# Attention of layer 0: exponentials first in ScalarE's round, conversions of the outputs last, projections in the rounds without a query

## The chip, the cores and the metric

The kernel runs on one core of one Trainium2 chip. A core has TensorE (PE, matrix multiplication), VectorE (DVE), ScalarE (ACT), GpSimd (POOL) and SyncE (SP, which issues transfers). The metric is the device time of one execution in microseconds (us). Each engine works through its own list of instructions in the order in which they were written, and waits at semaphores for the others.

## The reference

Two transformer layers over 4 sequences of 256 tokens with 512 features. The change touches the attention of layer 0 alone:

```
q_c = x @ Wq_c.T + bq_c;          q = q_c @ Wq_up.T + bq_up            # 32 heads
kv_nope, kv_rope = split(x @ Wkv_c.T + bkv_c)
k_nope, v = split(kv_nope @ Wkv_up.T + bkv_up);  k = [k_nope, kv_rope]
attn = softmax(q @ k.T / sqrt(192))                                    # 256 x 256 per sequence and head
out  = sum over heads of (attn @ v) @ Wo.T + bo
```

After it come a layernorm, a gated feed-forward, a second attention and a second feed-forward, which stay as they are.

## The kernel before

`attention0_heads` computes the 32 heads (h), each for 4 sequences (b = 0 to 3). One pair of h and b is a step s = 4h + b, and one round handles one step, as a software pipeline: in round s every engine does work that belongs to steps s + 1, s, s - 1, s - 2 and s - 3. Each engine has its own `round_(h, b)`, and the order of the calls in it is the order of its instructions. There is no scheduler. A hardware loop repeats heads 2 to 30; heads 0, 1, 31 and the rounds behind the last head stand outside it.

What one step goes through:

- TensorE `scores(s)` writes the bank `bs` (two of them). VectorE `maxes` (L548) takes the negative row maxima, ScalarE `exps` (L492) two exponentials with their row sums.
- VectorE `inverse` (L553) takes the reciprocals, GpSimd `norm` (L462) multiplies, TensorE `turn` (L635) transposes into `bt` (two banks).
- ScalarE `probs` (L498) copies the high part out of `bt`, VectorE `probs` (L557) computes the low part `pt_lo`.
- TensorE `values` (L646) multiplies with the latent values into `bo`, of which there is one bank. Steps 0 and 1 of a head make one pair, steps 2 and 3 the next.
- ScalarE `outs` (L503) copies the high part of a finished pair, VectorE `outs` (L562) makes the low part. Only after that may `values` of the next pair overwrite `bo`: it waits for `s_olo`.
- TensorE `project` (L655, L657) adds the pair to the accumulator; SyncE duplicates a part of `o_hi` for it by DMA.

Two queries per head are made for two sequences each: `merge` (L601, L603) and its conversions (L529, L532, L483, L537) prepare one matrix for a head; TensorE `query` makes `bq`, ScalarE `query` (L487) the high part, VectorE `query` (L542) the low part, which `scores` waits for.

In every round VectorE begins with the reciprocals of step s - 1 and the maxima of step s. ScalarE ends its round with the exponentials of step s. In rounds 1 and 3 of a head both have the outputs of a finished pair ahead of `probs`; in round 3 VectorE also does one reduction for a later layer (L585, "part"). TensorE has `project` in rounds 1 and 3, and a `query` in the same rounds.

Of the kernel before, what the change touches and what calls it, by code (L numbers as in the profile page):

```python
# [46 lines left out]
NH = 32  # L47
# [17 lines left out]
def f32(ap):  # L65

    return ap.bitcast(F32)
# [17 lines left out]
def plain(eng, sem):  # L85


    eng.sem_inc(sem, 1)


def has(x, n):

    return not isinstance(x, int) or 0 <= x < n
# [236 lines left out]
def attention0_heads(nc, k, io, g, lat, acc, first):  # L330
# [10 lines left out]
    NS, NPAIR = NB * NH, 2 * NH  # L341
    with ExitStack() as ctx:
# [35 lines left out]
        def run(eng, round_):  # L378

            def head(h):  # L380
                for b in range(NB):
                    round_(h, b)

            head(0)
            head(1)
            with eng.Fori(2, NH - 1) as h:
                head(h)
            head(NH - 1)
            head(NH)
            round_(NH + 1, 0)  # L390
            round_(NH + 1, 1)

        with nc.Block() as block:
            @block.sync
# [40 lines left out]
            @block.gpsimd  # L435
            def _(pool):
                def rope_part(h):


                    pool.wait_ge(s_w, 16 * h + 16)  # L440
                    need(pool, s_glo, h)
                    need(pool, s_qlo, 2 * h)
                    plain(pool, s_tick)
                    pool.tensor_scalar(gm[:, :, KVL:P], rope, SCALE0, None, ALU.mult)
                    pool.tensor_scalar(gb[:, :], bcols[:, 1:2], SCALE0, None, ALU.mult).then_inc(s_gpool, 1)

                def split_wv(h):
                    pool.wait_ge(s_wv, 16 * h + 16)
                    need(pool, s_om, 2 * h)
                    plain(pool, s_tick)  # L450
                    pool.tensor_copy(wvs[0][:, :], wv[:, :]).then_inc(s_wvh, 1)
                    pool.wait_ge(s_wvh, h + 1)
                    plain(pool, s_tick)
                    pool.tensor_copy(wvs[1][0:KVL, :], wv[0:KVL, :]).then_inc(s_wvl, 1)
                    pool.wait_ge(s_wvl, 2 * h + 1)
                    pool.tensor_tensor(wvs[1][KVL:P, :], wv[KVL:P, :], f32(wvs[0][KVL:P, :]), ALU.subtract)\
                        .then_inc(s_wvl, 1)
                    pool.wait_ge(s_wvl, 2 * h + 2)

                def norm(s, b):  # L460
                    pool.wait_ge(s_inv, s + 1)
                    pool.tensor_tensor(pr[b][:, :, :], pr[b][:, :, :],  # L462
                                       rinv[b][:, :][:, :, None].to_broadcast([P, 2, S]), ALU.mult)\
                        .then_inc(s_norm, 1)

                def round_(h, b):
                    s = 4 * h + b
                    if has(s - 1, NS):
                        norm(s - 1, (b - 1) % 4)
                    if b == 0 and has(h + 1, NH):  # L470
                        rope_part(h + 1)
                    if b == 2 and has(h - 1, NH):
                        split_wv(h - 1)

                rope_part(0)
                run(pool, round_)

            @block.scalar
            def _(act):
                def merged(h):  # L480
                    act.wait_ge(s_graw, h + 1)
                    act.wait_ge(s_gpool, h + 1)
                    act.activation(gms[0][:, :, :], gm[:, :, :], ACT.Identity).then_inc(s_ghi, 1)  # L483

                def query(p, par):
                    act.wait_ge(s_qmm, p + 1)
                    act.activation(q[par][0][:, :], bq[:, :], ACT.Identity, bias=gb[:, :]).then_inc(s_qhi, 1)  # L487

                def exps(s, b):
                    act.wait_ge(s_max, s + 1)  # L490
                    for i in range(2):
                        m = act.activation(pr[b][:, i, :], bs[b % 2][:, i * S:(i + 1) * S], ACT.Exp,  # L492
                                           bias=nmax[b][:, i:i + 1], accum_out=rsum[b][:, i:i + 1])
                    m.then_inc(s_exp, 1)

                def probs(s, b):
                    act.wait_ge(s_tmm, s + 1)
                    act.activation(pt[b][0][:, :, :], bt[b % 2][:, :].rearrange("p (a n) -> p a n", a=2),  # L498
                                   ACT.Identity).then_inc(s_thi, 1)

                def outs(p, par):
                    act.wait_ge(s_pv, 2 * p + 2)
                    act.activation(o[par][0][:, :], bo[:, :], ACT.Identity).then_inc(s_ohi, 1)  # L503

                def round_(h, b):
                    s = 4 * h + b
                    if b == 0 and has(2 * h + 1, NPAIR) and not (isinstance(h, int) and h == 0):
                        query(2 * h + 1, 1)
                    if b == 2 and has(2 * h + 2, NPAIR):
                        query(2 * h + 2, 0)  # L510
                    if b % 2 and has(2 * h - 2 + b // 2, NPAIR):
                        outs(2 * h - 2 + b // 2, b // 2)
                    if b == 1 and has(h + 1, NH):
                        merged(h + 1)
                    if has(s - 2, NS):
                        probs(s - 2, (b - 2) % 4)
                    if has(s, NS):
                        exps(s, b)

                merged(0)  # L520
                query(0, 0)
                query(1, 1)
                run(act, round_)

            @block.vector
            def _(dve):
# [28 lines left out]
                def probs(s, b):  # L555
                    dve.wait_ge(s_thi, s + 1)
                    dve.tensor_tensor(pt[b][1][:, :, :], bt[b % 2][:, :].rearrange("p (a n) -> p a n", a=2),  # L557
                                      f32(pt[b][0][:, :, :]), ALU.subtract).then_inc(s_tlo, 1)

                def outs(p, par):  # L560
                    dve.wait_ge(s_ohi, p + 1)
                    dve.tensor_tensor(o[par][1][0:KVL, :], bo[0:KVL, :], f32(o[par][0][0:KVL, :]), ALU.subtract)\  # L562
                       .then_inc(s_olo, 1)

                def round_(h, b):
                    s = 4 * h + b
                    if has(s - 1, NS):
                        inverse(s - 1, (b - 1) % 4)
                    if has(s, NS):
                        maxes(s, b)  # L570
                    if b == 1 and has(h + 1, NH):
                        merged_raw(h + 1)
                    if b == 0 and has(2 * h + 1, NPAIR) and not (isinstance(h, int) and h == 0):
                        query(2 * h + 1, 1)
                    if b == 2 and has(2 * h + 2, NPAIR):
                        query(2 * h + 2, 0)
                    if b % 2 and has(2 * h - 2 + b // 2, NPAIR):
                        outs(2 * h - 2 + b // 2, b // 2)
                    if b == 1 and has(h + 1, NH):
                        merged_lo(h + 1)  # L580
                    if has(s - 2, NS):
                        probs(s - 2, (b - 2) % 4)
                    if b == 3 and has(h, NH):
                        dve.wait_ge(s_part, 16 * h + 16)
                        dve.tensor_reduce(g["mag"][:, bass.ds(h, 1)], part[:, :], AX, ALU.max,  # L585
                                          apply_absolute_value=True).then_inc(s_mag, 1)
# [8 lines left out]
            def _(pe):  # L595
# [64 lines left out]
                def round_(h, b):  # L660
                    s = 4 * h + b
                    if has(s + 1, NS):
                        scores(s + 1, 2 * h + (b + 1) // 2, (b + 1) % 4)
                    if b == 3 and has(h + 1, NH):
                        query(h + 1, 2 * h + 3, 1)
                    if b == 1 and has(h - 2, NH):
                        project(h - 2, 2 * h - 3, 1)
                    if b == 3 and has(h - 1, NH):
                        project(h - 1, 2 * h - 2, 0)
                    if has(s - 1, NS):  # L670
                        turn(s - 1, (b - 1) % 4)
                    if has(s - 3, NS):
                        values(s - 3, 2 * h + (b - 3) // 2, (b - 3) % 4)
                    if b == 0 and has(h + 1, NH):
                        merge(h + 1)
                    if b == 1 and has(h + 1, NH):
                        query(h + 1, 2 * h + 2, 0)
# [1198 lines left out]
```

## Time and profile before

| | |
|---|---|
| median of 3 runs | 1572.85 us (1572.0 to 1576.03) |
| the profiled execution | 1576.75 us |
| its span, first to last instruction | 1575.0 us |
| busy over the span | PE 95%, PEld 83%, DVE 70%, ACT 49%, POOL 31% |
| granted TensorE clock, mean | 0.982 of full speed |

The stage of the 32 heads lies between 41.6 us (its first exponential) and about 409 us. In the slices of the page, where each digit is the busy share of a fortieth of the span in tenths, it covers slices 2 to 10. TensorE is busy in nine tenths or more there, ScalarE and VectorE in seven to eight tenths. Rows of a timeline have the start, the duration, the engine, the line and the operation, and in brackets the idle time of the engine just before it and who ended it. The start of one instruction and that of the next on the same engine can lie closer together than the duration says, since they overlap; a chain is followed by starts.

### The profile page before, as it was taken

Reading aid. Unit: us, or ns where it says so; the run is one execution under the profiler, and the core shown is the slowest. Engines: PE = TensorE matmul, PEld = TensorE weight load, DVE = VectorE, ACT = ScalarE, POOL = GpSimd, SP = SyncE. Lnnn points to the kernel's source line nnn. Section 1 sums busy time; section 2 is a strip of 40 time slices with the busy share of each in tenths; the row PEclk is TensorE's granted clock in tenths of the full one; section 3 lists DMA queues with packets and bytes.
Section 4 is the critical chain, followed back from the end, with each engine's and each line's share of the span. In section 5 each row is a group of like instructions: output and inputs, shape, how many; then the busy total and the mean of one; then the engine's idle time right before and its main releaser. Section 6 shows DMA issues by size and latency. Waiting matters only on the chain. (4 is left out here: it accounts for less than half of the span.)

```text
span 1575.0 us, 29365 instructions
## 1 busy us (share of the span) xinstructions
PE 1496.1 (95%) x8993; PEld 1312.2 (83%) x8993; DVE 1099.8 (70%) x2790; ACT 767.7 (49%) x2153; POOL 484.6 (31%) x537
## 2 busy tenths in 40 slices
PE   6999999999689989999999999999999999999898
PEld 5888888888368777988888888888888888988776
DVE  3788888888576756676676666666666666666666
ACT  3777777777345534444434444344443444434421
POOL 3455555555230113123213213312311321320321
PEclk9999999999889999999999999999999999999999
DMA  4222222222245440110011011011011101100001
GB/s 159 66 69 74 71 73 73 73 73 69 69 121 154 127 160 1 54 55 24 29 53 53 0 53 53 0 53 53 11 42 53 46 7 53 53 0 14 1 14 41
DMA packets 47954, 88.60 MB, mean 56 GB/s; under 512 B 6064, under 2 KB 14768, under 8 KB 47920
## 3 DMA queue, kind: packets, MB, share of 16 engines
q1 hardware_dynamic: 47920, 88.16, 19.1%
q8 instruction: 19, 0.31, 0.1%
q14 instruction: 15, 0.12, 0.0%
HBM read 77.66 MB, written 2.10 MB: 51 GB/s over the span
## 5 line engine op out<-in xcount | busy, mean ns | idle before, releaser
L98 PE MATMUL c_bj<-g_xT_hi,b_w 128*128 128x512 f32 x512 | 214.7, 419 | 2.8 <-PEq L928 2.8
L99 PE MATMUL c_bj<-g_xT_lo,b_w 128*128 128x512 f32 x512 | 203.5, 397 | 0.0
L100 PE MATMUL c_bj<-g_xT_hi,b_w 128*128 128x512 f32 x512 | 203.1, 397 | 0.0
L462 POOL TENSOR_TENSOR h_pr<-h_pr,h_rinv 128x512 f32<-128x512 f32 x128 | 133.2, 1041 | 152.9 <-DVE h_rinv L553 150.4
L1146 POOL CAST b_w<-b_raw_q 128x512 fp32r<-128x512 f32 x32 | 20.5, 640 | 435.8 <-PE c_bj L100 435.8
L98 PE MATMUL c_bj<-b_w,g_xT_hi 128*128 128x256 f32 x512 | 143.4, 280 | 0.0
L99 PE MATMUL c_bj<-b_w,g_xT_hi 128*128 128x256 f32 x512 | 143.2, 280 | 0.0
L100 PE MATMUL c_bj<-b_w,g_xT_lo 128*128 128x256 f32 x512 | 142.7, 279 | 0.0
L1378 DVE TENSOR_TENSOR c_v_lo<-c_bj,c_v_hi 128x256 fp32r<-128x256 f32 x128 | 54.3, 424 | 94.0 <-ACT c_v_hi L1290 94.0
L1382 DVE TENSOR_TENSOR g_res<-c_bj,g_res 128x512 f32<-128x512 f32 x128 | 88.3, 691 | 45.4 <-PE c_bj L100 42.8
L492 ACT ACTIVATE h_pr<-h_bs,h_nmax 128x256 f32<-128x256 f32 x256 | 118.8, 475 | 2.1 <-DVE h_nmax L548 2.1
L1274 ACT ACTIVATE c_o<-c_bo 128x128 f32<-128x128 f32 x128 | 35.5, 278 | 171.7 <-PE c_bo L1492 171.7
L100 PEld LDWEIGHTS c_bj<-g_xT_hi,b_w 128*128 128x128 f32 x512 | 97.1, 190 | 23.3
L98 PEld LDWEIGHTS c_bj<-g_xT_hi,b_w 128*128 128x128 f32 x512 | 97.1, 190 | 20.6 <-issue 3.3
L99 PEld LDWEIGHTS c_bj<-g_xT_lo,b_w 128*128 128x128 f32 x512 | 97.6, 191 | 17.2
L1269 ACT ACTIVATE c_pt<-c_bt 128x384 fp32r<-128x384 f32 x128 | 62.9, 491 | 90.0 <-PE c_bt L1479 90.0
L1290 ACT ACTIVATE c_v_hi<-c_bj 128x256 fp32r<-128x256 f32 x128 | 49.2, 384 | 116.6 <-PE c_bj L100 116.6
L98 PE MATMUL c_bj<-b_w,c_oT_hi 128*128 128x512 f32 x256 | 100.9, 394 | 2.1 <-DVEq L1386 2.1
L100 PE MATMUL c_bj<-b_w,c_oT_lo 128*128 128x512 f32 x256 | 100.3, 392 | 0.0
L99 PE MATMUL c_bj<-b_w,c_oT_hi 128*128 128x512 f32 x256 | 100.2, 391 | 0.0
L98 PEld LDWEIGHTS c_bj<-b_w,g_xT_hi 128*128 128x128 f32 x512 | 96.3, 188 | 3.0
L99 PEld LDWEIGHTS c_bj<-b_w,g_xT_hi 128*128 128x128 f32 x512 | 96.4, 188 | 2.9
(265 smaller groups left out, 4639.4 us busy)
## 6 DMA issues: line engine op xcount, KB each, us to landing
f_wi<-in_w_ffn SPq DMA_DIRECT2D x66, 256.0 KB, 2.6
h_part<-in_w_ffn SPq DMA_DIRECT2D x32, 264.0 KB, 2.6
h_o_mix<-h_o_hi SPq DMA_DIRECT2D x64, 128.0 KB, 2.2
b_raw_q<-in_w_attn SPq DMA_DIRECT2D x32, 256.0 KB, 6.4
b_raw_k<-in_w_attn SPq DMA_DIRECT2D x32, 256.0 KB, 7.0
b_raw_v<-in_w_attn SPq DMA_DIRECT2D x16, 512.0 KB, 7.4
b_raw_o<-in_w_attn SPq DMA_DIRECT2D x16, 512.0 KB, 3.9
a_w<-in_w_head SPq DMA_DIRECT2D x32, 225.0 KB, 2.6
```

The lines of the kernel that those rows point to most:

```text
L98: pe.matmul(out, w[0], x[0], start=start, stop=False, skip_group_check=True)
L99: pe.matmul(out, w[0], x[1], start=False, stop=False, skip_group_check=True)
L100: return pe.matmul(out, w[1], x[0], start=False, stop=stop, skip_group_check=True)
L462: pool.tensor_tensor(pr[b][:, :, :], pr[b][:, :, :], rinv[b][:, :][:, :, None].to_broadcast([P, 2, S]), ALU.mult)\
L492: m = act.activation(pr[b][:, i, :], bs[b % 2][:, i * S:(i + 1) * S], ACT.Exp, bias=nmax[b][:, i:i + 1], accum_out=rsum[b][:, i:i + 1])
L1146: pool.tensor_copy(hi[:, :], self.raw[n][:, :]).then_inc(self.s_whi[n], 1)
L1269: act.activation(pt[0], bt[:, 0:3 * P], ACT.Identity).then_inc(s_thi, 1)
L1274: act.activation(o1[:, :], bo[t % 2][:, 2 * P:3 * P], ACT.Identity).then_inc(s_orest, 1)
L1290: act.activation(v[c][0][:, 2 * t + bank - 1, :], bj[bank][:, 0:2 * DV], ACT.Identity)\
L1378: dve.tensor_tensor(lo, bj[bank][:, 0:2 * DV], f32(hi), ALU.subtract).then_inc(s_jlo[bank], 1)
L1382: dve.tensor_tensor(res[:, j, :], bj[bank][:, :], res[:, j, :], ALU.add)\
```

## The change

ScalarE's round begins with the exponentials of its step and no longer ends with them. On ScalarE and VectorE the outputs of a pair come after `probs`. The projections of a head move one round later each: from round 3 and the next head's round 1 to rounds 0 and 2 (those without a `query`). GpSimd's `split_wv` moves from round 2 to round 3, and a third round is added behind the last head. No arithmetic is added or taken away.

```
@@ (the rounds behind the last head)
-            round_(NH + 1, 0)
-            round_(NH + 1, 1)
+            for b in range(3):
+                round_(NH + 1, b)
@@ GpSimd
-                    if b == 2 and has(h - 1, NH):
+                    if b == 3 and has(h - 1, NH):
                         split_wv(h - 1)
@@ ScalarE, round_(h, b)
+                    if has(s, NS):
+                        exps(s, b)
                     (query)
-                    if b % 2 and has(2 * h - 2 + b // 2, NPAIR):
-                        outs(2 * h - 2 + b // 2, b // 2)
                     (merged)
                     if has(s - 2, NS):
                         probs(s - 2, (b - 2) % 4)
-                    if has(s, NS):
-                        exps(s, b)
+                    if b % 2 and has(2 * h - 2 + b // 2, NPAIR):
+                        outs(2 * h - 2 + b // 2, b // 2)
@@ VectorE, round_(h, b)
-                    if b % 2 and has(2 * h - 2 + b // 2, NPAIR):
-                        outs(2 * h - 2 + b // 2, b // 2)
                     (merged_lo)
                     if has(s - 2, NS):
                         probs(s - 2, (b - 2) % 4)
+                    if b % 2 and has(2 * h - 2 + b // 2, NPAIR):
+                        outs(2 * h - 2 + b // 2, b // 2)
@@ TensorE, round_(h, b)
-                    if b == 1 and has(h - 2, NH):
-                        project(h - 2, 2 * h - 3, 1)
-                    if b == 3 and has(h - 1, NH):
-                        project(h - 1, 2 * h - 2, 0)
+                    if b % 2 == 0 and has(h - 2, NH):
+                        project(h - 2, 2 * h - 4 + b // 2, b // 2)
```

ScalarE inside the loop, rounds 2 and 3 of a head, before. L487 is a query, L492 the exponentials, L503 the outputs of a pair, L498 `probs`; the digit in a name is the buffer.

```order
L487 ACTIVATE h_q0_hi<-h_bq,h_gb 128x512 [waits a_q_mm]
L498 ACTIVATE h_pt0_hi<-h_bt0 128x512 [waits a_t_mm]
L490 REGISTER_ALU
L492 ACTIVATE h_pr2,h_rsum2<-h_bs0,h_nmax2 128x256 [waits a_s_max]
L492 ACTIVATE h_pr2,h_rsum2<-h_bs0,h_nmax2 128x256
L502 ISA
L503 ACTIVATE h_o1_hi<-h_bo 128x512 [waits a_pv]
L498 ACTIVATE h_pt1_hi<-h_bt1 128x512 [waits a_t_mm]
L490 REGISTER_ALU
L492 ACTIVATE h_pr3,h_rsum3<-h_bs1,h_nmax3 128x256 [waits a_s_max]
L492 ACTIVATE h_pr3,h_rsum3<-h_bs1,h_nmax3 128x256
```

The same two rounds now:

```order
L492 ACTIVATE h_pr2,h_rsum2<-h_bs0,h_nmax2 128x256 [waits a_s_max]
L492 ACTIVATE h_pr2,h_rsum2<-h_bs0,h_nmax2 128x256
L486 REGISTER_ALU
L487 ACTIVATE h_q0_hi<-h_bq,h_gb 128x512 [waits a_q_mm]
L498 ACTIVATE h_pt0_hi<-h_bt0 128x512 [waits a_t_mm]
L490 REGISTER_ALU
L492 ACTIVATE h_pr3,h_rsum3<-h_bs1,h_nmax3 128x256 [waits a_s_max]
L492 ACTIVATE h_pr3,h_rsum3<-h_bs1,h_nmax3 128x256
L498 ACTIVATE h_pt1_hi<-h_bt1 128x512 [waits a_t_mm]
L502 ISA
L503 ACTIVATE h_o1_hi<-h_bo 128x512 [waits a_pv]
```

The wait for the maxima (`a_s_max`) now stands ahead of `probs`, and the outputs stand behind it.

VectorE in the loop, rounds 2 and 3 of a head, before. L553 are the reciprocals, L548 the maxima, L562 the outputs, L557 `pt_lo`.

```order
L553 RECIPROCAL h_rinv1<-h_rsum1 128x2 [waits a_s_exp]
L547 REGISTER_ALU
L548 TENSOR_REDUCE h_nmax2<-h_bs0 128x2 [waits a_s_mm]
L541 REGISTER_ALU
L542 SCALAR_TENSOR_TENSOR h_q0_lo<-h_bq,h_gb,h_q0_hi 128x512 [waits a_q_hi]
L557 TENSOR_TENSOR h_pt0_lo<-h_bt0,h_pt0_hi 128x512 [waits a_t_hi]
L553 RECIPROCAL h_rinv2<-h_rsum2 128x2 [waits a_s_exp]
L547 REGISTER_ALU
L548 TENSOR_REDUCE h_nmax3<-h_bs1 128x2 [waits a_s_mm]
L562 TENSOR_TENSOR h_o1_mix<-h_bo,h_o1_hi 64x512 [waits a_o_hi]
L557 TENSOR_TENSOR h_pt1_lo<-h_bt1,h_pt1_hi 128x512 [waits a_t_hi]
```

Round 3 there now, from its reciprocals:

```order
L553 RECIPROCAL h_rinv2<-h_rsum2 128x2 [waits a_s_exp]
L547 REGISTER_ALU
L548 TENSOR_REDUCE h_nmax3<-h_bs1 128x2 [waits a_s_mm]
L557 TENSOR_TENSOR h_pt1_lo<-h_bt1,h_pt1_hi 128x512 [waits a_t_hi]
L562 TENSOR_TENSOR h_o1_mix<-h_bo,h_o1_hi 64x512 [waits a_o_hi]
```

On VectorE the exchange of L562 and L557 is all; reciprocals and maxima still open the round.

## Rows read from the trace of the kernel before

**Rows 1.** Busy time of each engine from the first exponential to the stage's end.
```profile
41.60:409.30 367.70, 342.99 (x2402) 309.05 (x2401) 297.95 (x634) 272.89 (x797) 188.27 (x286) 1.00 0.27 70
```
**Rows 2.** Instructions that touch h_pr: the exponentials, first and last start.
```profile
L492 ACT ACTIVATE h_pr<-h_bs,h_nmax x256: 457/474/508, 41.6 to 399.1; 128x256 f32<-128x256 f32 x128
```
**Rows 3.** Waits between 60 and 380 us: total, times, longest.
```profile
PEld h_bs L98 <- ACT h_pr L492: 21.3, 28, 0.8
```
**Rows 4.** Timeline of one head, round 3: ScalarE, VectorE and TensorE's first product.
```profile
308.28 0.22 ACT L492 ACTIVATION_READ_ACCUMULATOR h_pr<-h_bs,h_nmax 128x1 f32 x1
308.37 0.61 ACT L503 ACTIVATE h_o_hi<-h_bo 128x512 fp32r<-128x512 f32 x1
308.53 0.17 DVE L553 RECIPROCAL h_rinv<-h_rsum 128x2 f32<-128x2 f32 x1
308.55 0.39 PE L98 MATMUL h_bs<-a_kv_hi,h_q_hi 128*128 128x256 f32 x1 [0.56 <-ACT h_pr L492]
...
309.23 0.67 DVE L562 TENSOR_TENSOR h_o_mix<-h_bo,h_o_hi 64x512 fp32r<-64x512 f32 x1
...
309.83 0.67 DVE L557 TENSOR_TENSOR h_pt_lo<-h_bt,h_pt_hi 128x512 fp32r<-128x512 f32 x1
...
310.17 0.21 ACT L492 ACTIVATION_READ_ACCUMULATOR h_pr<-h_bs,h_nmax 128x1 f32 x1
...
310.43 0.68 DVE L585 TENSOR_REDUCE g_mag<-h_part 128x528 int32 x1
...
311.04 0.15 DVE L553 RECIPROCAL h_rinv<-h_rsum 128x2 f32<-128x2 f32 x1
```
**Rows 5.** The same timeline, a query on TensorE and round 2.
```profile
305.06 0.39 PE L98 MATMUL h_bq<-a_qa_hi,h_gm_hi 128*128 128x512 f32 x1
...
306.21 0.28 PE L98 MATMUL h_bs<-a_kv_hi,h_q_hi 128*128 128x256 f32 x1
...
306.41 0.69 ACT L487 ACTIVATE h_q_hi<-h_bq,h_gb 128x512 fp32r<-128x512 f32 x1 [1.24 <-PE h_bq L615]
...
307.00 0.59 ACT L498 ACTIVATE h_pt_hi<-h_bt 128x512 fp32r<-128x512 f32 x1
307.13 0.75 DVE L542 SCALAR_TENSOR_TENSOR h_q_lo<-h_bq,h_gb,h_q_hi 128x512 fp32r<-128x512 f32 x1 [1.14 <-ACT h_q_hi L487]
...
307.47 0.48 ACT L492 ACTIVATE h_pr<-h_bs,h_nmax 128x256 f32<-128x256 f32 x1
...
307.80 0.68 DVE L557 TENSOR_TENSOR h_pt_lo<-h_bt,h_pt_hi 128x512 fp32r<-128x512 f32 x1
```
**Rows 6.** The same timeline, round 1: the conversion of the merged matrix.
```profile
303.36 0.42 ACT L483 ACTIVATE h_gm_hi<-h_gm 128x256 fp32r<-128x256 f32 x1 [0.38 <-DVE h_gb L532]
...
303.69 0.58 ACT L498 ACTIVATE h_pt_hi<-h_bt 128x512 fp32r<-128x512 f32 x1
```
**Rows 7.** Timeline of head 0, where exponentials wait for the maxima.
```profile
48.23 0.17 DVE L553 RECIPROCAL h_rinv<-h_rsum 128x2 f32<-128x2 f32 x1
48.31 0.67 DVE L548 TENSOR_REDUCE h_nmax<-h_bs 128x2 f32<-128x512 f32 x1
...
49.01 0.47 ACT L492 ACTIVATE h_pr<-h_bs,h_nmax 128x256 f32<-128x256 f32 x1 [0.33 <-DVE h_nmax L548]
```
**Rows 8.** Timeline behind the last head: values that wait for the outputs.
```profile
403.29 0.68 DVE L562 TENSOR_TENSOR h_o_mix<-h_bo,h_o_hi 64x512 fp32r<-64x512 f32 x1 [2.36 <-ACT h_o_hi L503]
...
404.12 0.36 PE L646 MATMUL h_bo<-h_pt_hi,a_cs 128*128 128x256 f32 x1 [1.03 <-DVE h_o_mix L562]
...
404.66 0.35 PE L646 MATMUL h_bo<-h_pt_hi,a_cs 128*128 128x256 f32 x1
```
**Rows 9.** Stretches where TensorE was less busy, columns as in rows 1; clock last but two.
```profile
398.66:402.07 3.41, 1.71 (x13) 1.51 (x14) 2.26 (x5) 1.54 (x6) 1.22 (x2) 1.00 0.23 58
...
405.49:408.90 3.41, 1.30 (x4) 0.60 (x4) 0.68 (x1) 0.50 (x1) 0.00 (x0) 1.00 0.17 38
408.90:412.31 3.41, 2.74 (x5) 1.25 (x5) 0.33 (x2) 2.83 (x4) 0.00 (x0) 0.50 0.55 167
```

## The prediction

> **What bounds the kernel now.** I read the busy time of the stage first, then the waits in it, then the timeline of one head. Between 41.60 and 409.30 us TensorE is busy for 342.99 of 367.70 us at the full clock, VectorE for 297.95 and ScalarE for 272.89 [rows 1]. The first exponential of the stage starts at 41.6 us and the last step's at 399.1 [rows 2]: 357.5 us for 127 rounds, 2.815 us a round, 11.26 us a head. So TensorE carries the stage, and what it waits for is what a better order could give back. In the waits there is one such line: the weight load of `scores` waits for the exponentials once per head, 21.3 us over 28 heads, 0.76 us each [rows 3]. In the timeline it is round 3: the exponentials of round 2 end at 308.28 + 0.22 = 308.50, and the product starts at 308.55 [rows 4]. The exponentials are that late because they stand behind the query, which starts at 306.41, and `probs`, at 307.00 [rows 5]. This is the wait that exponentials in front take away. TensorE's own work is then 11.26 - 0.76 = 10.5 us a head.
>
> **The stall that goes.** With the exponentials in front and 0.45 us of projection moved into round 2, nothing of the 0.76 us need be left: at most 0.76 x 31.75 heads (127 rounds) = 24 us. This is the upper bound of the gain, and it is only had if the other engines keep up.
>
> **What the new order adds.** Look at what stands between two maxima on VectorE. Its round is reciprocals, maxima of step s, (query or merged matrix), `pt_lo`, (outputs, part). `pt_lo` waits for ScalarE's `probs`. Before, ScalarE did `probs` ahead of the exponentials, so VectorE could do the maxima and go on to `pt_lo` while ScalarE was at its exponentials. Now `probs` stands behind the exponentials, and these wait for the maxima of the same round. So within each round the work is serial: maxima, exponentials, `probs`, `pt_lo`, and only then the next round's reciprocals and maxima. That the exponentials of the next step could start earlier does not help, for their maxima are queued on VectorE behind `pt_lo`.
>
> That a queue is held like this is in the trace: the exponentials of round 3 end at 310.17 + 0.21 = 310.38, and their reciprocals start at 311.04, behind the reduction of "part" that started at 310.43 [rows 4]. The Trainium skill (TensorE: Matmul & The Clock Gate, section on the array's architectural detail) says that ScalarE and VectorE are strict first-in, first-out and TensorE alone reorders, and then only weight loads. By that rule this row is general, and no instruction passes the waiting one; by the opposite the sum would be the gain above. The row agrees with the rule.
>
> **The links**, each from one start to the next:
> - reciprocals to exponentials through the maxima: 49.01 - 48.23 = 0.78 [rows 7]
> - exponentials to the next operation on ScalarE: 308.37 - 307.47 = 0.90 [rows 4, 5]
> - `probs` to `pt_lo`: 0.60 and 0.03 for the semaphore, as from the query's end (306.41 + 0.69 = 307.10) to its low part at 307.13 [rows 5]: 0.63
> - query to its low part: 307.13 - 306.41 = 0.72; low part to `pt_lo`: 307.80 - 307.13 = 0.67 [rows 5]
> - merged matrix to `probs`: 303.69 - 303.36 = 0.33 [rows 6]
> - `pt_lo`, outputs and "part" to the next on VectorE: 0.60, 0.60 and 0.61 [rows 4]
>
> Round 3: 0.78 + 0.90 + 0.63 + 0.60 + 0.60 + 0.61 = 4.12 us. The outputs on ScalarE run beside `pt_lo` and add nothing.
> Round 0: 0.78 + 0.90 + 0.72 + 0.67 + 0.60 = 3.67. `probs` runs beside the query's low part.
> Round 1: 0.78 + 0.90 + 0.33 + 0.63 + 0.60 + 0.60 = 3.84.
> Round 2: as round 0, 3.67, and what the query on TensorE is late.
>
> **TensorE in the new order.** Here the outputs behind `probs` count. `values` of a new pair may start only when the low part of the finished pair is out, which is now the last thing in the same round. In round 1 this low part starts at 0.78 + 0.90 + 0.33 + 0.63 + 0.60 = 3.24 and `values` follow 404.12 - 403.29 = 0.83 later [rows 8], at 4.07; the query behind them 404.66 - 404.12 = 0.54 later, at 4.61; its result reaches ScalarE 306.41 - 305.06 = 1.35 later [rows 5], at 5.96, which is 5.96 - 3.84 = 2.12 in round 2. ScalarE is free at 0.78 + 0.90 = 1.68 there. So round 2 is 3.67 + 0.44 = 4.11.
> In round 3 `values` start at 2.91 + 0.83 = 3.74, while TensorE has been through scores, query and turn by about 2.3; it idles some 1.4 us there and about 2 us ahead of the `values` of round 1. All other waits of TensorE fall inside the 15.7 - 10.5 = 5 us a head in which it has nothing to do, the projections too, which are hidden in any round.
>
> **Sum.** 4.12 + 3.67 + 3.84 + 4.11 = 15.74 us a head instead of 11.26: +4.48 a head, x 31.75 = +142. Head 0 has no outputs and hardly any query to wait for: its four rounds are some 4 us shorter than this, and the last head, without merged matrix and queries, some 2 (0.33, and in round 2 about 1.1, in round 0 nothing): +136. The tail gains the outputs behind one `probs` (0.5). The extra round has only one projection in it, which existed before. SyncE's duplicates start later with the outputs, but their projections come a round later too, and `split_wv` has 5 us of slack a head: nothing for both. Sum so far +137.
>
> **The clock.** In the stage it was 1.00, 2.4 GHz [rows 1]. At the stage's end, where TensorE worked 1.71 of 3.41 us it stayed so; it worked 1.30 of 3.41 us and the next stretch ran at 0.50, which is 1.2 GHz [rows 9]. With 2 us of idleness ahead of the `values` of round 1 the new order is near this. What it costs on the path is the query behind them: 306.21 - 305.06 = 1.15 us [rows 5], becomes 2.3. The bounds are nothing and 1.15 x 31.75 = 37 us. The stretches with 1.7 stand nearer to the new order (10.5 of 15.7 us busy on average), so I take a sixth of the upper end, +6. The Trainium skill (TensorE: Matmul & The Clock Gate, Part 1) has the throttled state as the default that activity releases; by it alone I could not say which of the two holds here, and rows decide.
>
> 1576.75 + 137 + 6 = 1719.75 us for the profiled execution; the median of the runs shown lies 3.9 us below it, so I forecast 1716 us.
>
> **Rivals.**
> 1. *Faster*: VectorE and ScalarE keep ahead of TensorE, the stall of 0.76 goes and nothing takes its place: 1572.85 - 24 = 1549. For it: both are busy for a quarter less than the stage lasts [rows 1], and the exponentials could start before the query. It decides from the point where a round's serial chain is under 2.8 us; the shortest has 3.67. Against: the chain has only links that the trace shows.
> 2. *Only the outputs' wait bites*: VectorE somehow runs ahead, and TensorE loses the 1.4 and 2 us ahead of `values`, less the 0.76: 2.65 x 31.75 = +84, 1657. For it: the place of L503 and L562 is wrong for TensorE whatever the exponentials do. Against: the queue of rows 4.
> 3. *The clock falls in most heads*: the upper end of the term above, and a little more where turns and scores at 1.2 GHz become late: +137 + 37 to 60, 1746 to 1770. If TensorE stayed at 1.2 GHz throughout, its 10.5 us would be 21 a head, over the chain: (21 - 11.26) x 31.75 = +309, 1882. For it: idle stretches of 2 us. Against: busy phases of 3 us and more lie between them.
> 4. *The change doesn't do what it says*: the exponentials stand first but wait there, so nothing starts earlier; with the outputs unhurt the time would stay at 1573. It is true in its first half, and the outputs make the second half unlikely.
>
> **How the numbers follow.** Forecast 0.62 (own range 1695 to 1740: 0.2 us a round are 25 us). Clock in most heads 0.20, at 1.2 GHz throughout 0.03; outputs alone 0.08; faster 0.05; unchanged 0.02. What a measurement can tell is about 0.3%, 5 us. Faster 0.05, same 0.02, slower 0.93. The range 1680 to 1770 leaves out the end of the clock case, the outputs alone and the faster side.
>
> **What would show it.** The starts of L492 should lie 15 to 16.5 us apart per head. ScalarE should be idle ahead of L492 in every round, released by `h_nmax` L548 as in [rows 7], some 1 to 2 us a round, VectorE idle ahead of L557 or L542, released by ScalarE, and TensorE ahead of L646, released by `h_o_mix` L562, twice a head. The wait of L98 for L492 should be gone. I am wrong if L492 still waits for nothing and TensorE stays over 90% busy in the stage, or if the granted clock there is far below 1.

## The result, and the profile after

The changed kernel takes 1748.82 us (median of 4 runs, 1740.43 to 1756.14) against 1573.3: 11.1% more, ratio 1.1111 with a 95% interval of 1.1044 to 1.1179. The forecast was 1716 in a range of 1680 to 1770. The profiled execution took 1742.03 us, 165.3 more than that of before. The four runs lie in two pairs, 1740.43 and 1742.03, and 1755.61 and 1756.14, at mean granted clocks of 0.950, 0.949, 0.952 and 0.953; the trace is of the first pair, and what the other pair's 14 us are is open. All of the 165.3 us has been lost by the time the feed-forward begins: its first product starts at 431.54 us before and at 596.84 after, 165.3 later, and from there to the end both profiles go alike.

One row shows the stage of the heads, from its first exponential to its last. The columns are the length, the busy time of TensorE, its weight loads, VectorE, ScalarE and GpSimd with their counts, the granted clock, the busy share of the DMA engines and GB/s.

```profile
41.60:560.30 518.70, 409.17 (x2372) 344.75 (x2372) 286.81 (x626) 269.48 (x789) 185.07 (x278) 0.89 0.19 49
```

VectorE and ScalarE are busy for about as long as in [rows 1], whose row goes on for 10 us behind the last exponential, but the stage from the first exponential to the last is 161 us longer. Nobody is near its limit: TensorE is busy for 409 of 519 us. The exponentials, against [rows 2]:

```profile
L492 ACT ACTIVATE h_pr<-h_bs,h_nmax x256: 463/473/478, 41.4 to 560.3; 128x256 f32<-128x256 f32 x128
```

From the first to the last it is 518.9 us where it was 357.5: 16.34 us a head instead of 11.26. One exponential lasts as long as before. The waits between 60 and 500 us, with total, times and longest, in place of [rows 3]:

```profile
ACT h_pr L492 <- DVE h_nmax L548: 180.5, 106, 2.1
DVE h_q_lo L542 <- ACT h_q_hi L487: 122.7, 53, 3.6
PE h_bo L646 <- DVE h_o_mix L562: 62.2, 53, 1.5
...
DVE h_pt_lo L557 <- ACT h_pt_hi L498: 42.6, 27, 1.6
...
ACT h_q_hi L487 <- PE h_bq L615: 31.3, 27, 1.8
```

These are the links of the forecast: ScalarE waits for the maxima in every round, VectorE for ScalarE behind them, TensorE for the outputs twice a head. The wait of [rows 3] is not in this list any more. The timeline shows how one round 3 goes, in place of [rows 4]: from the second exponential of round 3 to the first one of the next head's round 0.

```profile
299.65 0.46 ACT L492 ACTIVATE h_pr<-h_bs,h_nmax 128x256 f32<-128x256 f32 x1
...
300.10 0.59 ACT L498 ACTIVATE h_pt_hi<-h_bt 128x512 fp32r<-128x512 f32 x1
...
300.57 0.60 ACT L503 ACTIVATE h_o_hi<-h_bo 128x512 fp32r<-128x512 f32 x1
...
300.72 0.69 DVE L557 TENSOR_TENSOR h_pt_lo<-h_bt,h_pt_hi 128x512 fp32r<-128x512 f32 x1 [1.57 <-ACT h_pt_hi L498]
...
301.33 0.67 DVE L562 TENSOR_TENSOR h_o_mix<-h_bo,h_o_hi 64x512 fp32r<-64x512 f32 x1
...
301.93 0.68 DVE L585 TENSOR_REDUCE g_mag<-h_part 128x528 int32 x1
302.15 0.36 PE L646 MATMUL h_bo<-h_pt_hi,a_cs 128*128 128x256 f32 x1 [0.72 <-DVE h_o_mix L562]
...
302.54 0.15 DVE L553 RECIPROCAL h_rinv<-h_rsum 128x2 f32<-128x2 f32 x1
...
302.61 0.66 DVE L548 TENSOR_REDUCE h_nmax<-h_bs 128x2 f32<-128x512 f32 x1
...
303.31 0.48 ACT L492 ACTIVATE h_pr<-h_bs,h_nmax 128x256 f32<-128x256 f32 x1 [2.13 <-DVE h_nmax L548]
```

VectorE stands idle for 1.57 us until ScalarE, which did its exponentials first, has done `probs`. Then it has `pt_lo`, outputs and "part" ahead of it, and only at 302.54 come reciprocals and maxima. ScalarE in turn has been idle for 2.13 us when it gets the maxima. ScalarE waits for VectorE in every round (106 times in the 27 heads of the list), and VectorE once a round for ScalarE, at L542, L557 or L537, before it gets on to the next maxima.

What the forecast sized wrongly stands in a stretch a little later. First two stretches with their granted clocks, then TensorE in the first of them:

```profile
307.90:314.72 6.82, 5.67 (x20) 4.79 (x21) 2.81 (x6) 3.56 (x11) 1.04 (x1) 0.50 0.22 53
320.00:344.00 24.00, 17.32 (x115) 14.54 (x115) 14.22 (x32) 13.33 (x39) 9.58 (x14) 1.00 0.21 55
```
```profile
307.97 1.11 PE L635 MATMUL h_bt<-g_ident,h_pr 128*128 128x128 f32 x4 [0.45 <-POOL h_pr L462]
...
310.16 0.58 PE L646 MATMUL h_bo<-h_pt_hi,a_cs 128*128 128x256 f32 x1 [1.08 <-DVE h_o_mix L562]
...
311.19 0.63 PE L98 MATMUL h_bq<-a_qa_hi,h_gm_hi 128*128 128x512 f32 x1
...
313.32 0.41 PE L98 MATMUL h_bs<-a_kv_hi,h_q_hi 128*128 128x256 f32 x1
```

At a granted clock of 0.50, 1.2 GHz, the values of round 1 take 1.03 us to the query (0.54 in [rows 8]) and the query 2.13 (1.15 in [rows 5]): 0.49 + 0.98 = 1.47 us more. The `turn` ahead of them (L635) is slow too. In the next head but one, at the full clock, the same two instructions are:

```profile
340.81 0.65 PE L635 MATMUL h_bt<-g_ident,h_pr 128*128 128x128 f32 x4 [0.45 <-POOL h_pr L462]
...
343.00 0.39 PE L646 MATMUL h_bo<-h_pt_hi,a_cs 128*128 128x256 f32 x1 [1.54 <-DVE h_o_mix L562]
```

So the wait ahead of `values` in round 1 is 1.54 us, not 2, and in the slow head the clock fell before it, when TensorE had waited 0.68 us ahead of `merge` (at 305.75) and 0.45 us ahead of `turn`. Of the 20 falls that made a head longer, the clock record of the trace has 12 at this place and 8 behind the wait, in the last of the values or in the query.

The rounds on ScalarE agree. These are the exponentials of rounds 2 and 3, first in this head, then in the next but one, at the full clock:

```profile
310.80 0.47 ACT L492 ACTIVATE h_pr<-h_bs,h_nmax 128x256 f32<-128x256 f32 x1 [1.52 <-DVE h_nmax L548]
...
316.32 0.47 ACT L492 ACTIVATE h_pr<-h_bs,h_nmax 128x256 f32<-128x256 f32 x1 [1.59 <-DVE h_nmax L548]
```
```profile
343.64 0.48 ACT L492 ACTIVATE h_pr<-h_bs,h_nmax 128x256 f32<-128x256 f32 x1 [1.52 <-DVE h_nmax L548]
...
347.70 0.48 ACT L492 ACTIVATE h_pr<-h_bs,h_nmax 128x256 f32<-128x256 f32 x1 [1.59 <-DVE h_nmax L548]
```

Round 2 takes 5.52 us in the one and 4.06 in the other. Of the 30 intervals between heads from head 1 on, 10 are 15.68 to 15.70 us long, 8 are 16.5 to 16.8 and 12 are 17.1 to 17.2.

### The profile page after: what moved, and what is told of

Its sections match the earlier page's. It is cut to its first block and busy times, and to the rows that moved or that the text cites. A ratio compares the mean times of both kernels' runs of the same rounds, so it can differ in the third digit from the quotient of the medians.

```text
span 1740.2 us, 29364 instructions
## 1 busy us (share of the span) xinstructions
PE 1568.9 (90%) x8993; PEld 1353.7 (78%) x8993; DVE 1092.8 (63%) x2790; ACT 768.3 (44%) x2153; POOL 485.1 (28%) x537
## 5 line engine op out<-in xcount | busy, mean ns | idle before, releaser
L492 ACT ACTIVATE h_pr<-h_bs,h_nmax 128x256 f32<-128x256 f32 x256 | 119.2, 470 | 216.2 <-DVE h_nmax L548 216.2
L646 PE MATMUL h_bo<-h_pt_hi,a_cs 128*128 128x256 f32 x256 | 83.0, 343 | 75.6 <-DVE h_o_mix L562 75.6
L542 DVE SCALAR_TENSOR_TENSOR h_q_lo<-h_bq,h_gb,h_q_hi 128x512 fp32r<-128x512 f32 x64 | 48.0, 751 | 147.0 <-ACT h_q_hi L487 147.0
L557 DVE TENSOR_TENSOR h_pt_lo<-h_bt,h_pt_hi 128x512 fp32r<-128x512 f32 x128 | 87.8, 686 | 57.5 <-ACT h_pt_hi L498 55.6
L646 PEld LDWEIGHTS h_bo<-h_pt_hi,a_cs 128*128 128x128 f32 x256 | 51.9, 203 | 91.5 <-DVE h_o_mix L562 48.5
L99 PEld LDWEIGHTS c_bj<-g_xT_lo,b_w 128*128 128x128 f32 x512 | 97.6, 191 | 17.2
L98 PE MATMUL c_bj<-b_w,c_oT_hi 128*128 128x512 f32 x256 | 101.0, 394 | 2.1 <-DVEq L1384 2.1
```

The source lines that it names most:

```text
L98: pe.matmul(out, w[0], x[0], start=start, stop=False, skip_group_check=True)
L99: pe.matmul(out, w[0], x[1], start=False, stop=False, skip_group_check=True)
L542: dve.scalar_tensor_tensor(out=q[par][1][:, :], in0=bq[:, :], scalar=gb[:, 0:1], in1=f32(q[par][0][:, :]), op0=ALU.add, op1=ALU.subtract)\
L646: m = pe.matmul(out, cs[:, 2 * b + kt, :], pt[b][j][:, kt, :], start=(b % 2 == 0 and kt == 0 and j == 0), stop=(kt == 1 and j == 1), skip_ ...
```

## The experiments

All were compared with the kernel before on the same chip. A ratio is that of the two, with its 95% interval; a time is the median. Us a head are intervals between the exponentials of round 0, in the steady heads; in the kernel before they are 11.35 (11.26 in [rows 2] is the mean with the shorter first heads).

**Exponentials last again.** The changed kernel without its first edit.

```
@@ ScalarE, round_ of the changed kernel
-                    if has(s, NS):
-                        exps(s, b)
                     ...
                     (outs)
+                    if has(s, NS):
+                        exps(s, b)
```

> The changed kernel with ScalarE's exponentials last in the round again; the outputs stay behind probs and the projections stay in rounds 0 and 2. Theory (the loss is the serial chain maxima, exponentials, probs, pt_lo in one round): the chain is gone, VectorE can do the maxima while ScalarE does probs; the low part of the outputs is out before TensorE gets to values, and the projections fill part of the 0.76 us that TensorE waited once a head: about 11.26 - 0.45 us a head, 1559 us (1552 to 1575). Rival (the place of the outputs alone stalls TensorE twice a head): it stays at +84, about 1657 us.

1617.82 us, ratio 1.0271 (1.0254 to 1.0288), 12.6 us a head. Of the 11% some 8 are gone, so the order of the exponentials is the large part. ScalarE's wait for the maxima is not in the list of waits any more. But the number was missed by 59 us: I had put the outputs down as harmless once the exponentials are last. The waits between 60 and 400 us name them:

```profile
PEld h_bo L646 <- DVE h_o_mix L562: 42.8, 27, 1.6
PE h_bo L646 <- DVE h_o_mix L562: 36.4, 27, 1.4
```

These are two views of one wait, once a head. In the timeline it is in round 1, where outputs now stand behind the merged matrix and `probs`:

```profile
309.06 0.42 ACT L483 ACTIVATE h_gm_hi<-h_gm 128x256 fp32r<-128x256 f32 x1 [2.00 <-DVE h_gb L532]
309.38 0.58 ACT L498 ACTIVATE h_pt_hi<-h_bt 128x512 fp32r<-128x512 f32 x1
...
309.86 0.59 ACT L503 ACTIVATE h_o_hi<-h_bo 128x512 fp32r<-128x512 f32 x1
...
310.60 0.67 DVE L562 TENSOR_TENSOR h_o_mix<-h_bo,h_o_hi 64x512 fp32r<-64x512 f32 x1
...
311.33 0.39 PE L646 MATMUL h_bo<-h_pt_hi,a_cs 128*128 128x256 f32 x1 [1.34 <-DVE h_o_mix L562]
```

**Exponentials first, alone.** The same two lines moved in the kernel before, and nothing else.

> The kernel before with one edit: the exponentials first in ScalarE's round. Theory: the same chain in rounds 0 and 3 (3.67 and 4.12), 0.78 + 0.90 + 0.48 + 0.33 + 0.63 + 0.60 = 3.72 in round 1, and round 2 3.67 since the outputs are early and the query is not held: 15.2 us a head, +124 and at most some 10 for the clock: 1697 to 1710 us. Rival (the outputs' place is what costs): TensorE is not held at values, and the time is at or under that of before, 1549 to 1573.

1702.62 us, 1.0809 (1.0788 to 1.083), within the range. The steady head takes 15.32 us, its rounds 0 to 3 3.67, 3.85, 3.67 and 4.12 against 3.67, 3.72, 3.67 and 4.12; the 0.13 us in round 1 are not explained. ScalarE's waits for the maxima are as in the changed kernel (60 to 400 us), and TensorE's wait for the outputs is short:

```profile
ACT h_pr L492 <- DVE h_nmax L548: 152.5, 89, 2.1
...
PE h_bo L646 <- DVE h_o_mix L562: 18.6, 34, 0.6
```

The clock falls here too, in 11 stretches within the heads, but only two of the 30 intervals from head 1 on are longer (15.77 and 16.73). These are the heads of the first two falls. The other nine falls begin in round 0, such as this one:

```profile
119.50:122.80 3.30, 3.30 (x15) 2.99 (x15) 1.98 (x7) 2.30 (x7) 1.36 (x3) 0.50 0.00 0
```

Its head takes 15.32 us like the others, so this fall cost nothing.

**TensorE filled where it waits.** The changed kernel with matmuls that add zero (the tile `zero` is filled by GpSimd at the start, not shown).

```
@@ TensorE, round_, ahead of values
+                    for _ in range({1: 6, 3: 3}.get(b, 0)):
+                        pe.matmul(acc[0][:, :], zero[:, 0:P], qb[:, 0:HALF], start=False, stop=False,
+                                  skip_group_check=True)
```

> The changed kernel with 6 more matmuls of 512 columns ahead of the values of round 1 and 3 ahead of those of round 3 (zero weights, added to an accumulator: nothing is changed by them), so that TensorE works where it waited. Theory (round 2 takes 5.15 us instead of 4.11 in the heads whose query runs at 1.2 GHz): the granted clock in the stage goes from 0.89 to about 1.00, every head takes 15.7 us as the undisturbed ones do, and the time falls by about 25 us to about 1718 in the profiled run. Rival (the excess over the forecast is something else, latency of the chain or memory access): the filler changes nothing or adds its own time, 9 x 0.23 us x 31.75 = 66 us at most, so 1743 to 1810.

1729.25 us, 1.0977 (1.0947 to 1.1006): more work, and less time than the changed kernel in any of its runs, which alone excludes the rival. The theory's number was not reached: 13 of the 30 intervals are still 16.8 us, and one is 16.2. So a second run with more:

```
-                    for _ in range({1: 6, 3: 3}.get(b, 0)):
+                    for _ in range({1: 7, 3: 4}.get(b, 0)):
                     ...
@@ ahead of merge(h + 1) in round 0
+                        for _ in range(3):
+                            pe.matmul(acc[0][:, :], zero[:, 0:P], qb[:, 0:HALF], ...)
```

> As the filled kernel, with 7 matmuls ahead of the values of round 1, 4 in round 3 and 3 ahead of merge in round 0 (there were 6, 3 and none, and the clock still fell in some heads, which took 16.8 us beside 15.67). Theory: with less idleness the falls go, all heads take 15.7 us, and the time is 1576.75 + 137 and a few us for the tail: 1712 to 1722. Rival (the long heads have another cause than TensorE's idleness): as many long heads as before, 1729 or more.

1713.92 us, 1.0887 (1.0871 to 1.0904). All heads from head 1 on take 15.68 to 15.74 us, and the stage keeps the full clock:

```profile
41.60:539.00 497.40, 466.10 (x2830) 382.16 (x2828) 289.71 (x632) 271.81 (x794) 187.18 (x283) 1.00 0.20 51
```

TensorE is busy for 57 us more than in the changed kernel's stage, and the kernel is 35 us faster than 1748.82. Between the two profiled executions it is 1742.03 - 1714.33 = 27.7 us, of which some 25 lie between the first exponential and the last. That is what the slowed clock cost, shown and not only argued; the other 7 us between the medians no trace shows.

**The maxima a step ahead.** The changed kernel, with VectorE taking the maxima of the next step ahead of `pt_lo`.

```
@@ VectorE, round_
-                    if has(s, NS):
-                        maxes(s, b)
                     (query)
+                    if has(s + 1, NS):
+                        maxes(s + 1, (b + 1) % 4)
                     (merged_lo, probs, outs)
```

> The changed kernel with VectorE's maxima of step s + 1 ahead of pt_lo of step s - 2 (before: the maxima of step s at the start of round s). ScalarE's exponentials then find their maxima ready. Theory: the link from pt_lo back to the maxima is cut, TensorE bounds the stage again, with some tenths of a us a head for the late outputs: 10.5 to 11.3 us a head, 1549 to 1573 us. Rival (the late outputs alone hold TensorE): still two stalls of 1.4 and 2 us a head, about 1657 us.

1666.47 us, 1.0584 (1.0566 to 1.0601), 13.8 us in the undisturbed heads. The theory is missed by 93 us, and the rival's number by 9. The edit gives back 82 us, but the stalls of the outputs stay, up to 1.9 us at a time:

```profile
PE h_bo L647 <- DVE h_o_mix L562: 54.9, 47, 1.9
PEld h_bo L647 <- DVE h_o_mix L562: 48.5, 23, 2.1
```

That the late outputs weigh so much more here than alone (35 us, below) comes from where the maxima now stand, behind the query's low part. Rounds 1 and 2 of an undisturbed head:

```profile
357.29 0.67 DVE L562 TENSOR_TENSOR h_o_mix<-h_bo,h_o_hi 64x512 fp32r<-64x512 f32 x1
...
358.01 0.39 PE L647 MATMUL h_bo<-h_pt_hi,a_cs 128*128 128x256 f32 x1 [1.87 <-DVE h_o_mix L562]
...
358.60 0.39 PE L98 MATMUL h_bq<-a_qa_hi,h_gm_hi 128*128 128x512 f32 x1
...
359.96 0.69 ACT L487 ACTIVATE h_q_hi<-h_bq,h_gb 128x512 fp32r<-128x512 f32 x1 [2.44 <-PE h_bq L616]
...
360.68 0.75 DVE L542 SCALAR_TENSOR_TENSOR h_q_lo<-h_bq,h_gb,h_q_hi 128x512 fp32r<-128x512 f32 x1 [2.65 <-ACT h_q_hi L487]
...
361.35 0.68 DVE L548 TENSOR_REDUCE h_nmax<-h_bs 128x2 f32<-128x512 f32 x1
...
362.06 0.47 ACT L492 ACTIVATE h_pr<-h_bs,h_nmax 128x256 f32<-128x256 f32 x1 [0.93 <-DVE h_nmax L548]
```

Outputs, values, query, its high and its low part, maxima, exponentials: one chain, by which round 2 takes 5.56 us. So this run cuts one link and ties another, and is no clean measure of either.

**Projections alone, outputs alone, and exponentials with projections.**

```
@@ projections alone: TensorE, round_ of the kernel before (split_wv at b == 3 and a third last round with it)
-                    (project at b == 1 and b == 3)
+                    if b % 2 == 0 and has(h - 2, NH):
+                        project(h - 2, 2 * h - 4 + b // 2, b // 2)
@@ outputs alone: ScalarE and VectorE, round_ of the kernel before
-                    (outs ahead of merged and probs)
+                    (outs behind probs)
@@ exponentials and projections: ScalarE and VectorE, round_ of the changed kernel
-                    (outs behind probs)
+                    (outs ahead of merged and probs)
```

> The kernel before with only the projections moved to rounds 0 and 2 (with split_wv a round later and the third round behind the last head). Theory: round 1 loses 0.45 us of TensorE work, so the query and with it the exponentials of round 2 come 0.45 us earlier, and the projection in round 2 lies where TensorE waited for them; 0.3 of the 0.76 us remain: 11.35 - 0.45 = 10.9 us a head, 1573 - 14 = 1559 us. Rival (the projections are hidden wherever they stand, or the wait only moves): 1573 us.

1566.15 us, 0.9951 (0.9937 to 0.9964): faster by 0.5%, clear of the noise, and less than forecast. A head takes 11.02 us, not 10.9. The wait is still there, 0.30 us once a head as expected, where [rows 3] had 0.76:

```profile
PEld h_bs L98 <- ACT h_pr L492: 8.8, 29, 0.3
```

> The kernel before with only the outputs behind probs, on ScalarE and VectorE. The run with the exponentials last took 12.62 us a head with one wait of TensorE for the low part of the outputs in round 1, 1.5 us. Theory: that is the outputs' place alone, behind the merged matrix and probs of round 1; the projection in round 1 lies beside this wait, so it is the same 12.6 us a head, 1617 us (1605 to 1625). Rival (it takes the moved projections as well, whose work round 1 lost): about 0.8 us a head more than before at most, 1573 to 1600.

1610.04 us, 1.0221 (1.0205 to 1.0236), 12.50 us a head, within the expected range. The outputs alone cost 35 us in the kernel before. TensorE waits for them once a head, 0.89 us (60 to 380 us):

```profile
PE h_bo L646 <- DVE h_o_mix L562: 22.2, 25, 0.9
```

With the projections moved as well (exponentials last again, above) it is 8 us more, not less, and this wait is 1.35 us: the projection that stood beside it has gone to round 0, which takes 4.30 us instead of 3.87, and that fits the 8 us, but no run shows it apart.

> The changed kernel with the outputs ahead of probs again, as in the kernel before; exponentials first and the projections moved. Theory (the serial chain through ScalarE and VectorE sets the round, and projections are hidden): the same 15.3 us a head as with the exponentials first alone, 1698 to 1708 us; the difference to the changed kernel, about 45 us, is then what the late outputs add, 0.4 us a head in the chain and the rest in the clock. Rival (the moved projections matter in this order too): off from 15.3 by 0.4 us a head, 13 us.

1707.04 us, 1.0835 (1.0818 to 1.0852), 15.32 us a head like the exponentials alone: where the serial chain sets the pace, moving the projections gives nothing. One of the 30 intervals is longer (16.19), where the changed kernel has 20; the place of the outputs is all that differs.

**Versions meant to beat both.** Exponentials first, with the links cut one by one: maxima ahead and outputs early, then the reciprocals of step s in round s, then the maxima ahead of the query in round 0; and, from the other side, the projections alone with the exponentials of round 2 ahead of `probs`.

```
@@ VectorE, round_ (maxima ahead, outputs early; ScalarE's outputs ahead of merged and probs too; maxes(0, 0) ahead of the first round)
-                    if has(s, NS):
-                        maxes(s, b)
                     (merged_raw, query)
+                    if b != 1 and has(s + 1, NS):
+                        maxes(s + 1, (b + 1) % 4)
                     (outs, moved here from behind probs; merged_lo)
+                    if b == 1 and has(s + 1, NS):
+                        maxes(s + 1, (b + 1) % 4)
                     (probs)
@@ then, reciprocals first
-                    if has(s - 1, NS):
-                        inverse(s - 1, (b - 1) % 4)
+                    if has(s, NS):
+                        inverse(s, b)
@@ then, maxima before the query's low part
+                    if b == 0 and has(s + 1, NS):
+                        maxes(s + 1, (b + 1) % 4)
                     (query)
-                    if b != 1 and has(s + 1, NS):
+                    if b > 1 and has(s + 1, NS):
                         maxes(s + 1, (b + 1) % 4)
@@ the other side: ScalarE, projections alone
+                    if b == 2 and has(s, NS):
+                        exps(s, b)
                     (probs)
-                    if has(s, NS):
+                    if b != 2 and has(s, NS):
                         exps(s, b)
```

> A version meant to be faster than both: exponentials first on ScalarE, projections in rounds 0 and 2, the maxima of step s + 1 ahead of pt_lo on VectorE (in round 1 behind the low part of the merged matrix), and the outputs ahead of probs as in the kernel before. Theory: neither the serial chain nor the late outputs are left, nothing holds TensorE, and the stage goes at its own work: 10.5 to 10.9 us a head, 1549 to 1560 us. Rival (exponentials first cost something that is neither of the two): it stays well above 1573.

1585.81 us, 1.0071 (1.0057 to 1.0085), 11.6 us a head. Most of the loss is gone with both links, but the kernel is still above 1573, as the rival had it: "nothing holds TensorE" fell. From the timeline, a query round:

```profile
299.80 0.47 ACT L492 ACTIVATE h_pr<-h_bs,h_nmax 128x256 f32<-128x256 f32 x1 [0.63 <-DVE h_nmax L548]
...
300.27 0.47 ACT L492 ACTIVATE h_pr<-h_bs,h_nmax 128x256 f32<-128x256 f32 x1
...
303.45 0.15 DVE L553 RECIPROCAL h_rinv<-h_rsum 128x2 f32<-128x2 f32 x1
```

The second exponential starts at 300.27 and its reciprocals at 303.45: the query's low part, for which VectorE waits 1.15 us, the maxima and `pt_lo` lie between, and behind the reciprocals come GpSimd and the turn.

> The version with the maxima ahead and the outputs early (1586 us, 11.6 us a head) with one more edit on VectorE: the reciprocals of step s at the start of round s, since ScalarE's exponentials of step s now come first in that round; they stood a round later, about 2.5 us behind the exponentials' end, behind the query's low part, the maxima and pt_lo. Theory: TensorE waited at turn for norm, and norm for these late reciprocals; with them early the turn finds its input ready, and a head takes 10.6 to 11.0 us: 1551 to 1566 us. Rival (another thing holds TensorE there, such as bank or DMA waits): 1580 or more.

1580.94 us, 1.0047 (1.0033 to 1.0061), 11.43 us a head. The wait of the turn (L638) for GpSimd left the list of waits, so that wait was real, but its removal gave 5 us, not 20 to 35, and the time is where the rival had it. ScalarE still waits for the maxima in three rounds of four (60 to 380 us):

```profile
ACT h_pr L492 <- DVE h_nmax L548: 81.6, 84, 1.0
```

> As the one before, with the maxima ahead of the query's low part in round 0, where the scores are ready first. Theory: ScalarE's exponentials of round 1 no longer wait for them; TensorE is the bound already, so within 3 us of the one before. Rival (the exponentials' chain still bounds): faster than the one before by 0.3 to 0.6 us a head, 10 to 19 us.

1604.85 us, 1.0182 (1.0165 to 1.0199). Both expectations missed: it is 24 us slower than the one before. The wait for the query's low part in GpSimd's part of the merged matrix went from 62.0 us to this:

```profile
POOL h_gm L444 <- DVE h_q_lo L542: 88.0, 26, 3.4
```

That the later low part holds `merge` and round 1 behind it fits this row; I did not test it apart.

> The version with only the projections moved (1566 us) and in round 2, behind the query, ScalarE's exponentials ahead of probs. Theory: the exponentials of round 2, which TensorE still waits for by 0.3 us once a head, come 0.47 us earlier; pt_lo of that round comes 0.9 us later, which holds the next reciprocals by about 0.7 us, a turn that has some slack: 10.7 to 11.0 us a head, 1556 to 1566 us. Rival (the same serial chain as in the changed kernel, in one round of four): the late reciprocals hold norm and turn, and the time is above 1566, by up to 31.75 x 0.9 = 29 us.

1584.63 us, 1.0065 (1.0051 to 1.008), 11.60 us a head, 18.5 us above the projections alone: the rival. Exponentials ahead of `probs` in a single round of four make VectorE wait for `probs`, a line that neither the kernel before nor the projections alone have:

```profile
DVE h_pt_lo L559 <- ACT h_pt_hi L498: 17.5, 27, 0.7
```

The fastest kernel of all is the one with the projections alone, 0.5% under the kernel before.

## Why the prediction was right, and what it missed

**The number.** 1748.82 us lies in the stated range of 1680 to 1770, but outside the 1695 to 1740 that the forecast called its own and gave 0.62. It lies where rival 3 has it, 1746 to 1770, "the clock falls in most heads", which had 0.20, though the falls cost 25 us in the profiled execution and not its 37 to 60. The mechanism of the forecast is what happened, and the range covered a term that it had sized too small.

**The serial chain** was right in its place and its sizes. Its rounds, from starts of L492, are in the median 3.68, 3.82 and 4.13 us for rounds 0, 1 and 3, forecast 3.67, 3.84 and 4.12. With the clock kept up, round 2 takes 4.06 us, forecast 4.11, and the head 15.69, forecast 15.74. The chain appears with the exponentials' edit alone (15.32) and goes with it (12.6). ScalarE's and VectorE's waits are those forecast; the starts of L492 are 16.34 us a head apart in the mean, in the forecast's 15 to 16.5, but 20 of the 30 intervals lie above it.

**The outputs** were right as a link that holds `values`, and as a rival they were priced too high. Alone they cost 35 us, not 84: only round 1 stalls, 0.89 us, for in round 3 the query lies ahead of `values`. In the changed kernel TensorE waits for them twice, 1.54 us in round 1 where the forecast had 2; in the chain they add 0.37 us a head (15.69 against 15.32). They also bring most of the falls of the clock: 20 long heads against one without them. That the falls come in the gap ahead of the query, as the forecast had it, is not what the trace shows; 12 of 20 come ahead of that gap.

**The clock** is the term that was mis-sized. "I take a sixth of the upper end, +6" should have been about 25: in 20 of 30 intervals the head is 0.8 to 1.5 us longer, 25.2 us together. The price of one such head was too low as well, for not only the query (0.98 us) runs at 1.2 GHz but also the values ahead of it (0.49): 1.47 us where the upper end had 1.15. The choice went by two stretches at the stage's end [rows 9] and TensorE's busy share in the mean of a head. These rows were too few for it: in the changed kernel the clock fell behind waits of 0.68 and 0.45 us, and in the kernel with the exponentials last it stayed up in 28 of 30 heads beside a wait of 1.35. What exactly makes it fall is open. The sentence drawn from the Trainium skill (TensorE: Matmul & The Clock Gate, Part 1), that the throttled state is the default and activity releases it, agrees with the filled run, where added work alone brings the stage to 1.00.

**The tail** was forecast at +0.5 and took 4.1 more: from the last exponential to the feed-forward's first product 36.5 us, before 32.4 (431.54 - 399.1). Of this, 3.7 lie ahead of the last projection, which starts 12.87 us behind the last exponential where it was 9.17; TensorE waits there twice for outputs, 1.64 and 1.62 us, and once before, 1.03. How the rest of it divides I have not taken apart.

**The gain that was to be had** came only in part, and from the projections, which the forecast put down as hidden "in any round". In the changed kernel this holds; in the kernel before they give back 8.6 us.

**The parts do not add up**, and need not. In medians against the kernel before: exponentials first +128.5; outputs late +35; projections -8.6; that would be 155. All three together are +139 with the clock kept up, and +175.5 without. Beside the chain of the exponentials the late outputs are mostly hidden and the projections wholly.

The sum for the changed kernel: 137 forecast, 165.3 measured in the profiled execution; 25.2 of it lie in the heads whose clock fell and 3.6 in the tail beyond the 0.5, which leaves 136.5. Some of this closeness is luck: head 0 was 3.2 us shorter than the others where 4 were forecast, the last one 1.4 where 2 were, and each round 2 at full clock 0.05 shorter. The forecast also took 399.1 in [rows 2] for the first exponential of the last step; it is the second, 0.4 us later, which is so on both sides and changes nothing.

## What to carry to other kernels

Before an operation goes to the front of an engine's round, follow the round on both engines: if what it waits for is made at the start of the other engine's round, and the other engine's round ends with something made behind it, each round becomes the sum of both. Such a sum can be worked out from starts in the timeline: here to within 0.05 us a round in the changed kernel, and 0.13 in one round of another. When a change gives TensorE new waits of half a us to 1.5 us in each iteration, price what lies on the path behind them at the lower clock too, and don't give this case a small chance because TensorE's mean share of busy time looks high. And do not add up the prices of edits that were measured alone.

## What the hardware showed

Added work made the kernel faster: 14 matmuls of 512 columns a head that change nothing took the granted clock of the stage from 0.89 to 1.00 and the time from 1748.82 to 1713.92 us. In heads 2 to 30 of the changed kernel the clock fell in 19 of 29, though TensorE never waited longer than 1.55 us at a time. With the exponentials first alone, falls in round 0 of nine heads cost nothing (15.32 us a head with and without); in the changed kernel those in and behind round 1 cost 0.8 to 1.5 us each. The median of one exponential was 473 ns against 474 before.
